# Added bfloat16 products on TensorE in the first half of a delta-rule scan and in the first norms' chain

## What is computed

```python
def step(H, inp):
    k_t, v_t, q_t, a_t = inp
    pred = jnp.einsum('bk,bkv->bv', q_t, H)
    err = jnp.sum((v_t - pred) ** 2, axis=-1, keepdims=True)
    surprise = jax.nn.sigmoid(err / (SURPRISE_TEMP + 1e-06))
    kH = jnp.einsum('bk,bkv->bv', k_t, H)
    delta = k_t[:, :, None] * (v_t - kH)[:, None, :]
    a = a_t[:, :, None]
    H = a * H + (1.0 - a) * (surprise[:, :, None] * delta)
    y_t = jnp.einsum('bk,bkv->bv', q_t, H)
    return (H, y_t)
...
y = norm(scan(step)) @ Wo.T
x = x + ga * y
h = layernorm(x) * (1 + cb) + sb
x = x + gb * ffn0(h)      # ternary weights, silu gate; then layer 1 in the same form
```

## Time and profile before

| what | us |
|---|---|
| median of 3 runs | 1300.75 |
| the three runs | 1300.65, 1300.75, 1305.39 |
| the profiled execution, whole time | 1301.84 |
| its span, first to last instruction | 1299.9 |
| scan, first half (chunks 0 to 3) | 126.0 to 256.9 |
| meeting of the engines and prefix | 256.9 to 305.2 |
| tiles | 305.2 to 1299.9 |

### The profile page before, as it was taken

How to read it: one execution, slowest core, us unless ns; L and a number is a source line. 1 busy time by engine, 2 the same in 40 slices (tenths; PEclk the granted TensorE clock), 3 DMA queues, 4 the chain that set the end, 5 groups by cost and what they waited for, 6 DMA issues and landing times. The chain is left out here.

```text
span 1299.9 us, 13519 instructions
## 1 busy us (share of the span) xinstructions
PE 1135.4 (87%) x4632; PEld 602.2 (46%) x4632; DVE 873.2 (67%) x1602; ACT 524.2 (40%) x1091; POOL 169.7 (13%) x143
## 2 busy tenths in 40 slices
PE   5666879868999779989798988899998999989997
PEld 5423658645656334434344434344443444434443
DVE  3557775554666757879857886768887577883554
ACT  2433554324544236634326425236543163341421
POOL 3000000001111122211112112122301000110100
PEclk9667575556988889989899998999999999999999
DMA  7511111041222013323213001112120001100000
GB/s 219 176 33 33 43 39 49 1 162 49 83 81 81 1 48 113 116 58 111 71 50 95 24 25 57 41 33 87 40 65 9 1 21 63 47 32 1 1 33 32
DMA packets 47525, 75.57 MB, mean 58 GB/s; under 512 B 8321, under 2 KB 16001, under 8 KB 47329
## 3 DMA queue, kind: packets, MB, share of 16 engines
q1 hardware_dynamic: 47168, 74.62, 18.0%
q0 software_dynamic: 288, 0.09, 0.1%
HBM read 66.16 MB, written 8.54 MB: 57 GB/s over the span
## 5 line engine op out<-in xcount | busy, mean ns | idle before, releaser
L1560 PE MATMUL g_g<-h,wt 128*128 128x512 f16 x1728 | 410.6, 387 | 11.7 <-PEq L2440 6.7
L1560 PEld LDWEIGHTS g_g<-h,wt 128*128 128x128 bf16 (+1 forms) x1728 | 170.1, 99 | 236.0 <-issue 50.0
L1574 PE MATMUL g_d<-wt,parts 128*128 128x512 bf16 (+1 forms) x864 | 208.4, 383 | 7.9 <-DVE tmp L1672 3.5
L1483 PE MATMUL g_o<-shared 128*128 128x512 f32 x384 | 182.8, 620 | 16.3 <-ACT hf L2052 9.4
L2144 ACT ACTIVATE parts<-hid 128x512 f16<-128x512 f32 x108 | 68.1, 630 | 318.5 <-DVE hid L1842 313.0
L1835 DVE SCALAR_TENSOR_TENSOR hid<-th,g_g 128x512 f32<-128x512 f32 x108 | 73.6, 682 | 168.8 <-ACT th L2137 168.8
L1574 PEld LDWEIGHTS g_d<-wt,parts 128*128 128x128 f16 x864 | 84.0, 99 | 119.8 <-issue 23.0
L1483 PEld LDWEIGHTS g_o<-shared 128*128 128x128 f32 x384 | 75.2, 199 | 101.0 <-issue 73.9
L2251 POOL TENSOR_TENSOR acc<-acc,sqh 128x512 f32<-128x512 f32 x52 | 77.5, 1489 | 334.1 <-ACT sqh L2150 334.1
L1847 DVE TENSOR_TENSOR parts<-hid,parts 128x512 f16<-128x512 f32 x108 | 82.9, 768 | 31.9 <-ACT parts L2144 31.6
L1492 PE MATMUL g_o<-shared 128*128 128x512 f32 x128 | 64.2, 649 | 10.2 <-DVE shared L1919 5.2
(11 more groups left out here) (312 smaller groups left out, 1649.8 us busy)
## 6 DMA issues: line engine op xcount, KB each, us to landing
shared<-in_w SPq DMA_DIRECT2D x48, 256.0 KB, 2.7
x<-in_codes SPq DMA_DIRECT2D x32, 264.0 KB, 3.1
w_raw<-in_wt SPq DMA_DIRECT2D x16, 512.0 KB, 3.7
x<-in_wmod SPq DMA_DIRECT2D x7, 1024.0 KB, 5.2
wmod<-in_wmod SPq DMA_DIRECT2D x5, 1024.0 KB, 10.7
codes_f<-x SPq DMA_DIRECT2D x32, 132.0 KB, 1.7
gates<-in_x SPq DMA_DIRECT2D x4, 1024.0 KB, 5.8
x<-in_x SPq DMA_DIRECT2D x4, 1024.0 KB, 6.2
```

The source lines that it names most:

```text
L1483: mm = nc.tensor.matmul(dst[:], w1[:, n % 4, k], xmix[:, w, k], start=(k == 0), stop=(k == KD - 1))
L1560: mm = nc.tensor.matmul(pg[i][:], wide[:, k, o:o + P], h16[f % 2][:, s, k], start=(s == 0 and k == 0), stop=(s == 1 and k == KD - 1))
L1574: mm = nc.tensor.matmul(pd[j][:], parts16[:, t % 3, s, j * P:(j + 1) * P], wd[:, m, :], start=(m == 0 and s == 0), stop=(done and s == 1))
```

## The change

In `head` a new helper makes one product of `groupmean` (128 x 128, bfloat16, stationary) against one weight block `wt[:, 0]` (128 x 512, bfloat16) into the whole bank `own[b]`. It is issued ahead of the residual products of every round r > 0, and only the residual products that overwrite part of the bank are ever read. For this the wait for `res_out[b]` (VectorE has read the bank) is moved ahead of the helper, while the wait for the gated rows stays behind it. In `groups`, `scan_unit` makes two such products ahead of the residual products in the rounds r = 1 to 4 of chunk 4 alone. That is 4 x 4 x 2 = 32 products in the head and 4 x 2 = 8 in the prefix. Nothing else is changed; no other engine gets or loses an instruction.

```diff
+        def filled(b):
+
+            nc.tensor.matmul(own[b][:], groupmean[:], keep["wt"][:, 0], start=True, stop=True)
+
         def residual(n, r, b):
             t = b * NC + n
+            if n or r:
+                pe.wait_ge(res_out[b], n * R + r)
+            if r:
+                filled(b)
             if r == 0:
                 pe.wait_ge(kt_out, ORDER.index(t // NJ) * NJ + n % NJ + 1)
                 pe.wait_ge(h_out[b], n + 1)
             else:
                 if r == 1:
                     pe.wait_ge(l_out, ORDER.index(t // NJ) * NJ + n % NJ + 1)
                 pe.wait_ge(w_ready[b], n * R + r)
-            if n or r:
-                pe.wait_ge(res_out[b], n * R + r)
             for kind in range(2):
...
         def scan_unit(n, r):
             w = scan["w"]
             if r < R:
                 dst, full = take("res", n, r)
+                for _ in range(2 if n == HC and r else 0):
+                    nc.tensor.matmul(dst[:], keep["groupmean"][:], keep["wt"][:, 0], start=True, stop=True)
                 if r:
                     pe.wait_ge(w_ready, ROUNDS + round_no(n, r))
```

## The result

The changed kernel took 1309.05 us in the median of 10 runs (1306.32 to 1312.9), the kernel before 1302.67 beside it (1300.53 to 1305.46). The ratio is 1.005, with an interval from 1.0035 to 1.0066: slower by about half a per cent, and inside the predicted range. The profiled execution took 1306.32 us, the quickest of the ten, with a span of 1304.3, against 1301.84 and 1299.9 before. All medians here are of the runs in the chip's fast state: two runs of the experiments, of 1522.44 and 1324.49 us, fell into a slower state that has nothing to do with the kernel, and are left out.

The account below looks back on a forecast made before the run. TensorE at 1.2 GHz was taken to set the pace in chunks 2 and 3. 1301.84 + 9.75 (head) + 0.86 (prefix) - 3.3 (clock) = 1309.15 us, 1308.1 against the median; forecast case 1304 to 1311, wide range 1290 to 1313.

Parts of the forecast that it names:

- The total: Whole kernel: 1309.15 us against the profiled execution, 1308.1 against the median of the runs.
- What bounds the kernel: In chunks 2 and 3 TensorE sets the pace at 1.2 GHz; chunks 0 and 1 are shared with VectorE.
- The price of a product: Each added product costs 0.43 us at clock 0.50 and 0.23 us at 1.00, read from the mean's rows.
- How many lie on the path: Of the head's 32 products, 20 count at 0.43 us and 5 at 0.23 us: 9.75 us.
- the seven hidden ones: Head products said to cost nothing, by TensorE's waits or VectorE's lateness: two in chunk 0, two in chunk 1, three in chunk 2.
- The other 25: Head products said to cost their whole price: six in chunk 0, six in chunk 1, five in chunk 2, eight in chunk 3.
- The moved wait: Head: the wait for `res_out`, moved ahead, was already passed before the gated rows' wait in every round; zero cost.
- The prefix: Pairs ahead of r = 2, 3 and 4 fit in waits; only the pair ahead of r = 1 costs, 0.86 us.
- The clock: Wide products bring earlier or longer high clock: 1.7 us, 0.5 in the stretch ending at 175.5, 1.1 in chunks 2 and 3; together 3.3.
- The first (slack, 1301): Rival: the added products vanish in TensorE's idle time over the four chunks, 1300.75 to 1303 us; chance 0.20.
- The second (clock held, 1292): Rival: wide products hold the clock at 2.4 GHz in chunks 2 and 3, 1288 to 1297 us; chance 0.25.
- The third (the clock gives nothing): Rival: the sum without its clock term, 1311.4 us, range 1311 to 1318; chance 0.15.

Follow-up runs that it names:

- the prefix alone: Only the prefix's four pairs of products added to the kernel before, none in the head: 1304.37 us, ratio 1.0008 (0.9987 to 1.0028).
- the head alone: Only the head's 32 products, without the prefix's pairs, against the kernel before: 1309.30 us against 1302.81, ratio 1.0051 (1.0030 to 1.0071).

## Why the prediction was right, point by point

**The total.** The forecast was 7.3 us above the kernel before (1308.1 against 1300.75, the median of three runs); measured were 6.4 (1309.05 against 1302.67, the median of ten beside it). The mechanism, products that lengthen the path of an engine that has no slack, is what the traces show. The split over the parts is less good than the total, as follows.

**What bounds the kernel.** Right: in chunks 2 and 3 TensorE's own work at 1.2 GHz sets the pace, since their length moved with the clock (33.98 us at 0.55, 36.82 at 0.50) while VectorE's busy time stayed at 19.8.

**The price of a product.** Right where other work than a section stands ahead: in the changed kernel one starts at 138.05 and its residual at 138.47 (0.42), as these rows of TensorE's timeline show. Behind a section it was 0.24; the sum took 0.43 everywhere, and that a residual behind a section is itself slower (1.03 us, not 0.88) was overlooked.

```profile
138.05 0.63 PE L669 MATMUL sc<-wt,groupmean 128*128 128x512 bf16 x1
138.47 0.95 PE L689 MATMUL sc<-shared,LT 128*128 128x64 f32 x4
```

**How many lie on the path.** Five of the seven hidden ones cost nothing, and one of the two in chunk 1 cost 0.43 us, in an execution whose clock had fallen before it; in time the seven can't be told from nothing. The other 25, alone, were not run. Chunk 3 is the cleanest place, eight at 0.50 in both kernels: all eight count, as said, and 3.44 us forecast are 2.86 measured, for the three behind sections. Idle time before means was of no use to the change, as said: 10.1 us of it stand there afterwards, and the kernel that fills just that idle time gained.

**The moved wait.** Zero, as forecast (ratio 0.9999).

**The prefix.** The direction was right and the size too large: 0.45 us instead of 0.86. Rounds r = 2 to 4 of chunk 4 in TensorE's timeline after:

```profile
282.31 1.97 PE L1435 MATMUL g_o<-shared 128*128 128x64 f32 x8 [2.05 <-DVE shared L1713]
...
290.94 1.97 PE L1435 MATMUL g_o<-shared 128*128 128x64 f32 x8 [1.99 <-DVE shared L1713]
...
294.90 1.97 PE L1435 MATMUL g_o<-shared 128*128 128x64 f32 x8 [0.45 <-DVE shared L1713]
```

The waits of 3.11, 3.05 and 1.66 us shrank by 1.06, 1.06 and 1.21 and hide the pairs. The pair ahead of r = 1 was taken too dear: where the trace of the prefix alone has both of its records, it takes 0.83 us (267.26 to 268.09), but the residual behind it takes 1.74 us to the output products instead of 1.90 (267.36 to 269.26 before). Where the last 0.2 us went was not traced.

**The clock.** This is the weakest step. What it gave can't be read apart from the price; price and clock together came close in this execution (6.65 us for the forecast 6.45), less so in the head alone (8.36), and the parts did not. In chunk 0 it rose 5.8 us sooner (and once more before that), as said, but fell ahead of the states and outputs, so that their low stretch grew from 6.8 to 10.2 us. Chunk 1, where I had 0.5 us of gain, became 3.10 us longer instead of 1.1. Chunk 2 had its one short rise, at 197.0 us, in which a section ran 1.6 us faster; it got shorter by 0.92 us where I had about 2 more for its five products. Chunk 3 had no rise. That the misses cancel is luck: the head alone, with the same instructions there, had chunk 2 longer by 1.93 us and a rise in chunk 3, and chunk 1 differs by as much between executions of the same work. What the medians confirm is the total.

**The rivals.** The first (slack, 1301) falls: 1309.05 us, and VectorE's waits grew. The second (clock held, 1292) fell for this kernel: chunks 2 and 3 were at 0.55 and 0.50. Its mechanism is real, though. It appeared in part with two and three products per residual, and in the medians it paid off only where the products stood in waits for casts. I had written that of the idle time before the means "nothing can be used". That was true of the change and too narrow a thought on the kernel: 18 wide products fit into the 9.1 us there, and brought the clock up. The three covered ones of chunk 2 were as free, and by themselves did nothing to the clock. The third (the clock gives nothing) would be 1311.4 / 1300.75 = 1.0082 of the kernel before, above the interval's end of 1.0066, and the rises at 132.2, 145.8, 180.0 and 197.0 us speak against it, though little work stood behind the first and the third; the forecast's 1308.1 is 1.0057 of it, inside.

## What to carry to other kernels

Wide filling products were free here only where the engine really waited for another one: look, place by place, whether a wait stands on that very row of the timeline. Behind a queue of real work each cost 0.24 to 0.43 us at 1.2 GHz, and the engines that waited for this one waited longer. What brought the clock up without loss here were wide products in the longest waits ahead of slow work; a twin with narrow ones in the same places shows whether it is the clock. And before a difference of a stage is explained, compare two traces in which that stage is the same work: here they differed by up to 3 us in a chunk.

## What the runs showed of the hardware that was not expected

- A product of 64 columns ahead of a float32 pair cost 0.22 us at 0.50, one of 512 columns 0.43; behind a section of 2-column products they cost 0.04 and 0.24. In both places eight times the columns made 0.2 us, and the rest of the price depended on what stood ahead.
- 18 products of 512 columns in waits moved the clock and the time (1296.59 us); 18 of 64 columns in the same waits moved neither (1301.88 us).
- With the same instructions, chunk 1 of the scan took 27.29 or 25.40 us, chunk 2 with the added products 35.06 or 37.91, and the tiles these, at the same mean clock:

Windows of the tiles, first before, then after:

```profile
303.64:1299.90 996.26, 917.89 (x3796) 439.57 (x3794) 701.50 (x1122) 403.12 (x745) 145.30 (x104) 0.95 0.17 51
```

```profile
309.69:1304.30 994.61, 913.53 (x3757) 438.13 (x3794) 700.88 (x1122) 403.14 (x745) 145.47 (x104) 0.95 0.17 51
```

The kernel with wide products in the waits gave back 3.5 us in its tiles (999.80 us); whether that is such a difference or a consequence of its earlier start stays open.
